# Moving the weight quantization out of the second attention pass, reordering its transposes and its projections, and swapping casts and squares between ScalarE and VectorE

## The reference

```python
nx = layernorm(x) * gamma + beta
q, k = softmax over each head's 64 columns of (nx @ Wq.T + bq), (nx @ Wk.T + bk)
v = nx @ Wv.T + bv
A = einsum('bnhd,bnhl->bhdl', k, v)            # per sequence and head, over all tokens
x2 = layernorm(x + x @ Wh.T + bh + einsum('bnhd,bhdl->bnhl', q, A))
quantize(W) = clip(round(W / (mean(|W|) + 1e-5)), -1, 1)
h = relu(x2 @ quantize(W1).T + b1)             # 4096 wide
out = layernorm(x2 + h @ quantize(W2).T + b2)
```

## Time and profile before

| | |
|---|---|
| median of 5 runs | 9852.31 us (9847.88 to 10412.41) |
| profiled execution | 9857.09 us, span 9855.5 us on core 2; the cores' spans are 9820.1 to 9855.5 |
| busy share | TensorE matmuls 77%, weight loads 44%, VectorE 37%, ScalarE 16%, GpSimd 1% |
| granted TensorE clock, core 2 | 0.884 |
| DMA | 26 GB/s on the mean; loads of W pieces land 4.3 us after their issue |

### The profile page before, as it was taken

One profiled execution on the slowest core, in us unless ns is written; L12 is line 12 of the kernel. 1 busy time (PEld: TensorE's weight loads), 2 busy tenths in 40 slices (PEclk: granted clock), 3 DMA queues, 4 the chain that ended last, 5 costly groups with the idle time before them and its releaser, 6 DMA issues.

```text
span 9855.5 us, 121885 instructions; the slowest of 8 cores (9820.1 to 9855.5 us)
## 1 busy us (share of the span) xinstructions
PE 7608.7 (77%) x45395; PEld 4375.8 (44%) x46099; DVE 3608.8 (37%) x6063; ACT 1620.1 (16%) x2493; POOL 144.4 (1%) x276
## 2 busy tenths in 40 slices
PE   2788878887666666676674189899999999999998
PEld 1333333333333333333332165556666666666665
DVE  5455554443333333333333322222222222222222
ACT  1111111111211211111111011111111111111111
POOL 0000000000000000000000000000000000000000
PEclk9998989888888888888886599999999999999999
DMA  1111110000000010000001100000000000000000
GB/s 60 56 48 45 50 33 18 18 16 16 26 29 32 26 33 28 32 26 28 33 26 43 49 12 18 18 18 18 18 18 14 14 18 18 18 18 18 18 18 9
DMA packets 74486, 259.69 MB, mean 26 GB/s; under 512 B 12303, under 2 KB 12455, under 8 KB 73902
## 3 DMA queue, kind: packets, MB, share of 16 engines
q1 hardware_dynamic: 36526, 117.57, 4.2%
q0 software_dynamic: 37376, 134.28, 3.8%
HBM read 184.67 MB, written 67.12 MB: 26 GB/s over the span
## 4 chain that ended last, share of the span: by engine, by line
PE 71%; DVE 16%; issue 4%; DMA 4%; ACT 2%; DVEq 1%; ACTq 0%; POOL 0%; POOLq 0%; SPq 0%
PE P_K L64 26%; PE P_V L64 25%; PE P_A L64 9%; PE P_SP L64 9%; DVE B L64 5%; DVE ar L64 4%; DVE sm L64 4%; DMA ar<-W 3%; PE P_T L64 3%; DVE a L64 3%; ACT a L64 1%; DVEq L60 1%; ACT L64 1%; DVEq L63 0%; DVE AW L64 0%
## 5 line engine op out<-in xcount | busy, mean ns | idle before, releaser
L64 PE MATMUL P_K<-AW,a 128*128 128x512 bf16 x6016 | 1514.6, 413 | 112.8 <-DVE a L64 105.4
L64 PE MATMUL P_T<-id,ar 128*128 128x128 f32 x3328 | 569.4, 321 | 1282.8 <-DVE ar L64 1132.2
L64 DVE CAST B<-ar 128x256 bf16<-128x256 f32 (+1 forms) x1152 | 390.0, 339 | 2658.6 <-PE P_K L64 2538.5
L64 PE MATMUL P_V<-AW,a 128*128 128x512 bf16 x6016 | 1341.6, 379 | 20.3 <-issue 20.3
L64 PE MATMUL P_K<-AW,B 128*128 128x512 bf16 x3840 | 1037.6, 385 | 177.5 <-DVE B L64 164.7
L64 PEld LDWEIGHTS P_T<-id,ar 128*128 128x128 f32 x3328 | 448.3, 166 | 1415.5 <-issue 1409.2
L64 PEld LDWEIGHTS P_K<-AW,a 128*128 128x128 bf16 x6144 | 632.4, 106 | 953.3 <-issue 399.2
L64 PE MATMUL P_V<-AW,B 128*128 128x512 bf16 x3904 | 1046.0, 385 | 10.1
L64 PE MATMUL P_A<-a,AW 128*128 128x256 bf16 x8192 | 1008.7, 278 | 55.6 <-DVE a L64 55.6
L64 PE MATMUL P_SP<-a,AW 128*128 128x256 bf16 x8192 | 999.8, 276 | 0.0
L64 PEld LDWEIGHTS P_A<-a,AW 128*128 128x128 bf16 x8192 | 813.0, 99 | 274.3 <-issue 72.1
(11 more groups left out here) (62 smaller groups left out, 3104.8 us busy)
## 6 DMA issues: line engine op xcount, KB each, us to landing
ar<-x SPq DMA_DIRECT2D x128, 512.0 KB, 3.9
ar<-W POOLq DMA_DIRECT2D x128, 512.0 KB, 4.3
x2scr<-ar POOLq DMA_DIRECT2D x64, 512.0 KB, 4.9
ar<-x2scr SPq DMA_DIRECT2D x64, 512.0 KB, 3.9
out<-ar POOLq DMA_DIRECT2D x64, 512.0 KB, 4.7
ar<-Wk SPq DMA_DIRECT2D x8, 512.0 KB, 3.7
ar<-Wv SPq DMA_DIRECT2D x8, 512.0 KB, 3.6
ar<-Wq SPq DMA_DIRECT2D x8, 512.0 KB, 3.6
```

The costliest lines, as they stand in the source:

```text
L64: ins = getattr(h, meth)(*args, **kw)
```

## The change

1. `proj` no longer does one half of the columns after the other. For each of the 8 slices of the contraction it does high x high, high x low and low x high, and each for both halves in turn; the four bias matmuls come at the end. The count stays.
2. The Squares of `ln_stats`, of pass 2 and of `epi` become a multiplication on VectorE.
3. The casts of exp(k) and V in pass 1, and of the hidden slices in the feed-forward loop, go from VectorE to ScalarE.
4. In pass 2 `trans_pair2` of the next tile is emitted ahead of the 24 matmuls with A_sb.
5. The magnitude sums run one unit a tile over all 64 tiles of pass 1.
6. Pass 2 quantizes nothing. After it the 32 pieces of W1 and then the 32 of W2 are quantized in one stretch, with AR[8] and AR[3] as load buffers in turn on SyncE's queue, and AR[5], AR[6] and AR[7] for the compares and the result, in float32.

```diff
-            for nh in range(2):
-                first = True
-                for part, lhs in ((0, lhs_hi), (1, lhs_lo), (2, lhs_hi)):
-                    wslot = slot + (1 if part == 2 else 0)
-                    for kc in range(DC):
+            first = True
+            for kc in range(DC):
+                for ws_, lhs in ((slot, lhs_hi), (slot + 1, lhs_hi),
+                                 (slot, lhs_lo)):
+                    for nh in range(2):
                         last = sd.op("tensor", "matmul",
                                      out=dst_psum[:, nh * 512:(nh + 1) * 512],
                                      lhsT=lhs[:, kc * 128:(kc + 1) * 128],
-                                     rhs=wsl(wslot, kc, nh * 512, 512),
+                                     rhs=wsl(ws_, kc, nh * 512, 512),
...
+            for nh in range(2):
                 sd.op("tensor", "matmul", out=dst_psum[:, nh * 512:(nh + 1) * 512],
                       lhsT=ones16[pw:pw + 1, 0:128],
...
-            ev_sq = sd.op("scalar", "activation", out=tmp_ap, in_=src_ap,
-                          func=AF.Square, waits=waits + [need(("ar4", y))],
-                          inc="s")
+            ev_sq = sd.op("vector", "tensor_tensor", out=tmp_ap, in0=src_ap,
+                          in1=src_ap, op=ALU.mult,
+                          waits=waits + [need(("ar4", y))], inc="v")
...
-            ev_eh = sd.op("vector", "tensor_copy", out=ek16[:, 0:1024],
+            ev_eh = sd.op("scalar", "copy", out=ek16[:, 0:1024],
...
-            ev_vh = sd.op("vector", "tensor_copy", out=v16[:, 0:1024],
+            ev_vh = sd.op("scalar", "copy", out=v16[:, 0:1024],
...
+            if j + 1 < NT:
+                trans_pair2(j + 1)
             ev_y = None
             for c in range(DC):
                 for lo, ro in ((0, 0), (1024, 0), (0, 1024)):
...
             protect(("b16", 0), ev_y)
-            if j + 1 < NT:
-                trans_pair2(j + 1)
...
             emitB2(j)
-            prep_quant_unit(j)
...
+        def ffn_quant(ntiles, tile_ap, dst_quad, ev_c):
+            last = None
+            for t in range(ntiles):
+                wslot = 8 if t % 2 == 0 else 3
+                wb = AR[wslot]
+                ev_l = dma("sync", f"lw{t % 2}", wb[:, :], tile_ap(t),
+                           waits=[need(("ar", wslot))])
+                ev_pa = sd.op("vector", "tensor_scalar", out=AR[5][:, :],
+                              in0=wb[:, :], scalar1=c128[:, 0:1], scalar2=None,
+                              op0=ALU.is_gt,
+                              waits=[ev_l, need(("ar4", 1)), need(("ar", 5))] + ev_c,
+                              inc="v")
+                ev_pb = sd.op("vector", "tensor_scalar", out=AR[6][:, :],
+                              in0=wb[:, :], scalar1=negc[:, 0:1], scalar2=None,
+                              op0=ALU.is_lt, waits=[need(("ar", 6))], inc="v")
+                ev_wq = sd.op("vector", "tensor_tensor", out=AR[7][:, :],
+                              in0=AR[5][:, :], in1=AR[6][:, :],
+                              op=ALU.subtract,
+                              waits=[ev_pb, need(("ar", 7))], inc="v")
+                protect(("ar", wslot), ev_wq)
...
+                    bk, evt, n = trans_quad(srcs, id32[:], waits=[ev_wq])
+                    last = sd.op("vector", "tensor_copy",
+                                 out=dst_quad(t, q),
+                                 in_=PT[bk][:, 0:512].rearrange("p (a b) -> p a b", a=4),
+                                 waits=[evt], inc="v")
...
-            ev_hi = sd.op("vector", "tensor_copy", out=hT_hi(r),
+            ev_hi = sd.op("scalar", "copy", out=hT_hi(r),
```

More of the change, by code:

```diff
@@ L382, in proj @@
                                      lhsT=lhs[:, kc * 128:(kc + 1) * 128],
[L383 to L385 removed]
+                                     rhs=wsl(ws_, kc, nh * 512, 512),
+                                     start=(kc == 0 and ws_ == slot and lhs is lhs_hi),
+                                     stop=False, skip_group_check=True,
                                      waits=(waits if first else []), inc="pe")
                         first = False
+            for nh in range(2):
                 sd.op("tensor", "matmul", out=dst_psum[:, nh * 512:(nh + 1) * 512],
@@ L469, in gamma_unit @@
             return ev_a
[L471 to L518, removed]
-                bk, evt, n = trans_quad(srcs, id32[:], waits=[ev_wq])
-                last = sd.op("vector", "tensor_copy", out=dst_quad_fn(t, q),
-                             in_=PT[bk][:, 0:512].rearrange("p (a b) -> p a b", a=4),
-                             waits=[evt], inc="v")
-                protect(("pt", bk), last)
-            protect(("ar", 8), last)
-            return last
@@ L527, in w1_dst_quad @@
[L527 to L537 removed]
+        prep_gammas = ([("gW1", t) for t in range(FCN)] +
@@ L538, in build_nc, with run_gamma @@
                        [("gW2", t) for t in range(FCN)])
-        prep_quants = [("qW1", t) for t in range(FCN)]
-        def run_prep_unit(u):
+        def run_gamma(u):
             kind, t = u
@@ L773, in emitB2 @@
             protect("P_V", ev_r1)
-            ev_sq = sd.op("scalar", "activation", out=AR[4 + y][:, :],
-                          in_=AR[y][:, :], func=AF.Square,
-                          waits=[ev_r1, evt], inc="s")
+            ev_sq = sd.op("vector", "tensor_tensor", out=AR[4 + y][:, :],
+                          in0=AR[y][:, :], in1=AR[y][:, :], op=ALU.mult,
+                          waits=[ev_r1, evt], inc="v")
             ev_1 = sd.op("vector", "reduce_sum", out=c_s1(y), in_=AR[y][:, :],
@@ L942, in epi @@
                 protect(("PO", sub), ev_r2)
-                ev_sq = sd.op("scalar", "activation", out=AR[4 + y][:, :],
-                              in_=xs[:, :], func=AF.Square,
-                              waits=[ev_r2, need(("ar4", y))], inc="s")
+                ev_sq = sd.op("vector", "tensor_tensor", out=AR[4 + y][:, :],
+                              in0=xs[:, :], in1=xs[:, :], op=ALU.mult,
+                              waits=[ev_r2, need(("ar4", y))], inc="v")
                 ev_1 = sd.op("vector", "reduce_sum", out=c_s1(y), in_=xs[:, :],
```

131 lines of the change are left out of this document (77 added, 54 removed).

## The result

The changed kernel's median is 9549.7 us (9168.96 to 9669.94, 6 runs); beside it on the same chip the kernel before had 9961.25 (9843.78 to 10789.73, 10 runs). The ratio of the fast runs on record is 0.9719, 95% interval 0.9692 to 0.9746: faster by 2.8% (the medians differ by 4.1%), where 9020, or 8.4%, was forecast. 9549.7 lies far over the range's upper end of 9125. These ratios, and the medians, are those of the slowest core, and they hold stretches at a lower clock that come to some cores and not to others, in both kernels. They don't set like against like either: five of the ten executions of before took 9844 to 9852, as the profiled one with eight undisturbed cores did, while each of the 15 executions of the changed kernel whose cores are on record has a pair of cores over 40 us above 9005, the span of its undisturbed cores.

The account below looks back on a forecast made before the run. The prediction saw TensorE held back by pauses and the lowered clock after them, only the feed-forward being near full TensorE. Terms -830 - 99 - 25 - 3 + 44 + 77 + 3 = -833 took 9857.1 to 9024, forecast 9020; range 8870 to 9125.

Parts of the forecast that it names:

- three signs of being wrong: Clock in the two passes clearly off 0.85 to 0.9; VectorE wait ahead of q's transposes; projections over 11.6 at full clock.
- the one of slow projections: Rival: alternating PSUM halves lowers the clock in projections, 2862 us at worst, making the kernel slower; chance 0.02.
- Pass 2, -830: Pass 2: quantization leaves and next tile's transposes go ahead of the A matmuls; 2089 us against 2919.
- The pause of 8.5: Pass 2: from the start of q's transposes to the next projection, 8.5 us a tile instead of 10.39.
- The clock loss of 1.33 from pass 1: Pass 2: slower matmuls after each tile's pause, taken over from pass 1's mean, 1.33 us in the period of 32.7.
- the rival of the clock that stays up: Rival: shorter pauses in both passes keep the upper clock; 168 us less, to 8850; chance 0.15.
- The VectorE loop of 31.3: Pass 2: VectorE's work for a tile, Square included, takes 31.3 us, barely hidden under the period of 32.7.
- Pass 1, -99: Pass 1: two casts moved to ScalarE let P_A and the next Wk start 1.57 us earlier in 63 tiles.
- Joins, -25 in pass 1: Projections: fewer switches between full and one-row bias matmuls, 0.2 us each, 0.4 a tile; bounds nothing or 0.25.
- Quantization, +44: Between the passes and the feed-forward: W1 and W2 in 64 units of 6.1 us, 408 us in all, 44 more.
- Loads not hidden: Rival: quantization units wait for their loads, 11 us a unit; 314 us more, to 9335; chance 0.03.
- Feed-forward, +77: Feed-forward group boundaries: Squares on VectorE, less the moved cast, add 2.38 us at 31 boundaries and 2.76 at the end.

Follow-up runs that it names:

- the two kernels with zeros: Changed kernel and kernel before, each with attention weights, W1 and W2 overwritten by zeros: medians 9154.34 us and 9993.12 us.
- the kernel with the Squares back: Changed kernel with all Squares on ScalarE and the cast of h on VectorE, as before: median 9085.7 us, uncut cores 8813 to 8821.
- the better version: Changed kernel with all Squares and the cast of h on old engines, quantized weights copied from PSUM by ScalarE: medians 9178.92 and, on another chip, 9043.61 us.

## Why the prediction was wrong

The forecast of 9020 was 530 us too low against the median, and its mechanism was right for the most part: on one core, and between the two kernels with zeros, the change gives some 840 where 833 were to come. That these agree so closely is luck: on core 4 the stages miss their terms by +15 (pass 1), -49 (pass 2), -1 and +28 (feed-forward), which nearly cancel. Two of the three signs of being wrong that the prediction names have come: the clock in pass 2 is 0.96, outside 0.85 to 0.9, and VectorE is waited for ahead of q's transposes. Point by point:

- **The step that failed** is the one that carried the sum over from one execution to the time: "The profiled execution took 9857.1 (span 9855.5), so 9024; the median of the runs is 4.8 lower". That execution had eight uncut cores, and the median of the 5 runs lies 5 us beside it: the earlier trace rows show 0.89 and 0.95 of the clock in the stages with real work, and I took this for what the kernel has. The runs showed that in most executions some pair of cores spends hundreds to thousands of us at 0.80, in either kernel, and the slowest core is the measured time: beside this change before itself went from a median of 9852 to one of 9961, and to 10570, 9983, 10729, 10258 and 10608 on the chips of the experiments. The sum should have been a difference, with the time of the slowest core as an unknown above it. The hint stood in the times: 9847.88 to 10412.41, a tail of 560 us over the median (a second of the five took 10070.19), and the prediction named no rival for it. How much of the 530 is the chips' and how much comes because the changed kernel is cut more often than before isn't separated. None of its rivals could have given 9550 but the one of slow projections, for another reason.
- That the cut depends on the numbers multiplied is shown: with zeros throughout, 14 executions of two kernels without a cut core; with zeros in the attention part, none cut there in the profile. The Trainium skill says it ahead ("TensorE: Matmul & The Clock Gate", section "Seeing it yourself"): a limiter of peak current takes a die to 13/16 of the clock, 0.81, when three or more of its cores run dense matmuls, and operands that are all zero don't trip it. By that rule alone every core would have been at 0.81 throughout. The traces agree in the level (0.79 to 0.80) and in the zeros, and disagree in the extent: pairs of cores, for a part of the time, and on a neighbour pair of the same die not at all (cores 0/1 in pass 1, 2/3 from 7480 us, in the profile above). Which pairs, and when, is open.
- **Pass 2, -830**: measured -879 on core 4, and the stage is 2022 where 2089 was built. The pause of 8.5 is there, and two terms are wrong in opposite ways. "The clock loss of 1.33 from pass 1, whose tile has a similar pause" isn't there: the P_K projection behind the pause takes 10.31 for 47 matmuls, as P_V's (it was the rival of the clock that stays up, for this stage alone; in pass 1 the loss is there, 1.6). The VectorE loop of 31.3, held to be hidden under 32.7, is what TensorE waits for now; with its Square taken away the span is 66 us shorter (pass 2 at 1964 to 1968 against 2022 to 2049). 27 of these us are the wait itself, and a pause shorter by 0.35 a tile makes some 22.
- **Pass 1, -99**: the P_A wait is 3.29 instead of 4.87, as predicted; the stage gave 112 in all. Two terms of it were put at nothing or nearly: the move of the sums of |W| and of the quantization alone gave 9 (3 were booked), and the Square on VectorE, held to "fit in", costs 12, as the kernel with the Squares back shows; so the casts must have given some 110, which no run shows alone. **Joins, -25 in pass 1**: 3. The P_V projection got the 0.2 shorter that was booked, P_K longer by nearly as much, so the lower bound, nothing, was close.
- **Quantization, +44**: +43. **Loads not hidden**: no wait for a load in the rows of the changed kernel above. **Feed-forward, +77**: +105. From the g matmuls to the end of the pause a boundary took 15.42 us (7107.89 to 7123.31) and takes 18.02 (7105.91 to 7123.93), 2.60 where 2.38 were booked; the matmuls after it take 0.9 more. 105 / 31 is 3.4. That slow matmuls come with a longer pause was left out of the term. The 7.6 us expected ahead of the first P_K matmul are 6.51, as much of the delay already stands ahead of P_V's bias matmuls (5.03 instead of 2.05).
- **Slow projections by alternating order**: not seen; undoing it gave 3 us the other way.

## What to carry to other kernels

Predict a change as a difference on one core, and keep the slowest of eight cores apart: on this chip its time holds stretches at 0.80 of the clock that come with real data in any of these kernels, and that cost over 1100 us at the worst, more than the change gives. To measure a change free of them, compare cores whose windows show the full clock, or run both kernels once on zeros. When work is taken out of a stage, price what is moved to another engine against the period that the stage will have if its other terms come out well: the Square that was booked at nothing in pass 2 cost 66 us.

## What the hardware showed that I had not expected

Cores fall to 0.80 in pairs, and independently: in one execution of the better version (the last profile of it) cores 2 and 3 were at 0.80 for some 1300 us of pass 2, 4 and 5 through all of it, and the other four never. Within a tile, a projection behind a pause of 9.6 us of transposes and small matmuls starts at full speed in pass 2 (10.31 for 47, in the tile shown above), and one behind the shorter pause of pass 1 (transposes, 3.29 of idleness, 1.50 of P_A matmuls) doesn't (11.92). What in the pause decides this I haven't tried.
